# First attention of a fused model: value products in groups of four and five key tiles, tail keys padded to 128 rows, tail queries' maxima moved beside the tail keys' scores

## The reference

```python
# per batch of 8: N = 1056 tokens, nh = 8 heads, dh = 8
qkv = (x @ qkv_w + qkv_b).reshape(Bw, Nw, 3, nh, dh)
q, k, v = (qkv[:, :, 0], qkv[:, :, 1], qkv[:, :, 2])
attn = jnp.einsum('bnhd,bmhd->bhnm', q * scale, k)
bias = jnp.transpose(rpb_table[rel_idx], (2, 0, 1))
attn = jax.nn.softmax(attn + bias[None], axis=-1)
out = jnp.einsum('bhnm,bmhd->bnhd', attn, v).reshape(Bw, Nw, Cd)
```

## Time and profile before

| | us |
|---|---|
| median of 3 runs | 2691.78 |
| lowest, highest | 2688.55, 2697.84 |
| time of the profiled execution | 2689.29 |
| its span in the trace | 2687.5 |
| the attention stage in it | about 369 to 1223 |
| TensorE busy, of the span | 2455.1 (91%) |
| VectorE busy | 1911.8 (71%) |
| ScalarE busy | 1437.0 (53%) |

### The profile page before, as it was taken

One profiled execution on the slowest core, in us unless ns is written; L12 is line 12 of the kernel. 1 busy time (PEld: TensorE's weight loads), 2 busy tenths in 40 slices (PEclk: granted clock), 3 DMA queues, 4 the chain that ended last, 5 costly groups with the idle time before them and its releaser, 6 DMA issues. The chain is left out here.

```text
span 2687.5 us, 51435 instructions
## 1 busy us (share of the span) xinstructions
PE 2455.1 (91%) x18136; PEld 1069.5 (40%) x18136; DVE 1911.8 (71%) x4910; ACT 1437.0 (53%) x2468; POOL 394.1 (15%) x489
## 2 busy tenths in 40 slices
PE   8987689999999999997799997987799998799999
PEld 3336523333333333335333333666544444433333
DVE  4566688889888889873577776659677774366665
ACT  2117637777777777772344443427666765144333
POOL 2002100000000000005111112132101002311110
PEclk9997779999999999996899999666699999599999
DMA  2114511101010101306100000245612241600110
GB/s 92 24 32 155 194 30 27 37 26 37 25 37 25 37 25 37 61 9 130 28 21 22 22 22 22 65 106 159 226 45 84 64 98 43 138 16 17 32 25 12
DMA packets 233520, 155.14 MB, mean 58 GB/s; under 512 B 187617, under 2 KB 192546, under 8 KB 233042
## 3 DMA queue, kind: packets, MB, share of 16 engines
q1 hardware_dynamic: 220098, 123.57, 17.2%
q0 software_dynamic: 10368, 19.06, 2.5%
q10 hardware_dynamic: 2808, 9.22, 1.5%
HBM read 86.75 MB, written 65.09 MB: 57 GB/s over the span
## 5 line engine op out<-in xcount | busy, mean ns | idle before, releaser
L1666 DVE TENSOR_REDUCE att_mpart<-ps 128x1 f32<-128x512 f32 x1024 | 633.7, 683 | 55.7 <-PE ps L1486 50.6
L1624 ACT ACTIVATE att_p<-ps 128x704 f32<-128x704 f32 x768 | 546.5, 760 | 214.8 <-PE ps L1551 207.8
L1580 PE MATMUL ps<-att_p,att_v 128*9 128x352 f32 x3072 | 300.7, 462 | 0.1
L1486 PE MATMUL ps<-att_kT,att_qT 64*128 64x512 bf16 x1024 | 281.2, 386 | 20.9 <-DMA att_qz<-qt_d 8.4
L1551 PE MATMUL ps<-att_qT,att_kT 64*128 64x352 bf16 x1536 | 251.5, 317 | 7.3 <-ACT att_p L1624 6.9
L1280 DVE TENSOR_REDUCE cau_mpart<-ps 128x1 f32<-128x512 f32 (+5 forms) x384 | 193.1, 552 | 81.1 <-PE ps L1106 61.1
L2418 ACT ACTIVATE mo_act<-ps,mo_b 128x768 f32<-128x768 f32 x176 | 156.3, 901 | 132.0 <-PE ps L2300 127.4
L2571 DVE TENSOR_TENSOR mo_g<-mo_act,ps 128x768 f32<-128x768 f32 x176 | 167.4, 951 | 77.3 <-PE ps L2335 41.2
L1247 ACT ACTIVATE cau_p<-ps 128x704 f32<-128x704 f32 (+6 forms) x272 | 171.6, 660 | 82.3 <-PE ps L1165 49.7
L2970 ACT ACTIVATE mo_act<-ps 128x1024 f32<-128x1024 f32 (+1 forms) x108 | 102.9, 953 | 195.9 <-PE ps L2884 195.6
L1551 PEld LDWEIGHTS ps<-att_qT,att_kT 64*128 64x128 bf16 x1536 | 82.0, 93 | 272.9 <-issue 263.2
(11 more groups left out here) (419 smaller groups left out, 3928.9 us busy)
## 6 DMA issues: line engine op xcount, KB each, us to landing
qt_d<-pre_qT SPq DMA_DIRECT2D x8, 1056.0 KB, 4.3
kt_d<-pre_kT SPq DMA_DIRECT2D x8, 1056.0 KB, 7.3
att_kT<-kt_d SPq DMA_DIRECT2D x32, 264.0 KB, 2.8
att_qT<-qt_d SPq DMA_DIRECT2D x32, 264.0 KB, 3.0
cqt_d<-cpr_qT SPq DMA_DIRECT2D x8, 1056.0 KB
cau_qT<-cqt_d SPq DMA_DIRECT2D x16, 528.0 KB, 4.1
o_d<-att_o POOLq DMA_DIRECT2D x128, 37.1 KB, 2.7
cv_d<-cpr_v POOLq DMA_DIRECT2D x16, 288.0 KB, 6.0
```

Of the source, the lines that this page charges most:

```text
L1486: mm = pe.matmul(ps[:, bank, :], qT[half(s), u, j * P:(j + 1) * P], kT[half(s), u, c * BANK:(c + 1) * BANK], start=True, stop=not near)
L1580: mm = pe.matmul(ps[32 * cg:32 * cg + DV, 7, 0:TH], v[:, u, i, s, :], p[:, r, s, :], start=i < 2, stop=i == FULL - 1)
L1624: e = act.activation(p[:, n % PRING, :, :], ps[:, bank:bank + 2, 0:TH], ACT.Exp)
L1666: red = dve.tensor_reduce(mpart[:, j, s, c:c + 1], ps[:, bank, :], AX.X, ALU.max)
```

## The change

Groups of value products become (0,1,2,3) and (4,5,6,7,tail): 6 in a pair in place of 15. The buffer `p` gets nine slots in place of four. The tail keys' values are multiplied over all 128 rows: `vt` gets 128 partitions, and its lower half, and that of the one slot of `p` that the tail uses, are set to zero once by GpSimd (`blank`). The maxima of the tail queries move: the first one to the entry before the tail unit of the first third, the other two to the entries before the tail unit of the second; the tail keys' two go to the end of the list. The entries of a tail unit now run ahead of its scores, not behind. The numbers of entries behind each unit are written out (`sides`). The loops over batches become one loop over all 32 pairs, in which scores run ahead of values, and the copy of a third is left pending, across the ends of batches too. The copy of a third comes behind the first exponential of the fifth unit of the next third.

```diff
-    QT, MRING, PRING = 2, 3, 4
+    QT, MRING, PRING = 2, 3, 9
...
-    groups = [(t, [(t, i) for i in part]) for t in range(3) for part in ((0, 1), (2, 3), (4, 5), (6, 7), (None,))]
+    groups = [(t, [(t, i) for i in part]) for t in range(3) for part in ((0, 1, 2, 3), (4, 5, 6, 7, None))]
...
-    maxes += [("keys", s, 0, 0) for s in range(2)] + [("query", 0, 0, c) for c in range(3)]
+    maxes.insert(21, ("query", 0, 0, 0))
+    maxes += [("query", 0, 0, c) for c in range(1, 3)] + [("keys", s, 0, 0) for s in range(2)]
...
-    cut = [len(side) * c // NU for c in range(NU + 1)]
+    sides = (2, 1, 2, 1, 1, 2, 1, 1, 2) * 2 + (2, 1, 1, 3, 1, 1, 1, 1, 2)
+    cut = [sum(sides[:c]) for c in range(NU + 1)]
...
-        vt = nm.sb("vt", [64, U, 2, DV])
+        vt = nm.sb("vt", [P, U, 2, DV])
...
             pool.memset(mz[:, :, :, :], 0.0).then_inc(mz_set, 1)
+            pool.wait_ge(mz_set, 1)
+            pool.memset(vt[2 * TT:P, :, :, :], 0.0).then_inc(blank, 1)
+            pool.wait_ge(blank, 1)
+            pool.memset(p[2 * TT:P, PRING - 1, :, :], 0.0).then_inc(blank, 1)
+            pool.wait_ge(blank, 2)
...
-                    n = u * NU + first_unit[g] + c
-                    pe.wait_ge(p_made, it * U * NU + n - 1 if n >= 2 else it * U * NU)
+                    unit = first_unit[g] + c
+                    n = (it * U + u) * NU + unit
+                    if i is None:
+                        for pos in range(cut[unit], cut[unit + 1]):
+                            side_step(it, u, pos, last)
+                    at_least(pe, p_made, n - 1)
...
-                            mm = pe.matmul(ps[64 * s:64 * s + DV, 7, 0:TH], vt[:, u, s, :], p[0:2 * TT, r, 0, :], start=False,
+                            mm = pe.matmul(ps[64 * s:64 * s + DV, 7, 0:TH], vt[:, u, s, :], p[:, r, 0, :], start=False,
                                            stop=True)
...
+            start(0)
+            for k in range(pairs):
+                for g in range(NG):
+                    if g + 1 < NG:
+                        scores(k // U, k % U, g + 1, k >= pairs - U)
+                    elif k + 1 < pairs:
+                        start(k + 1)
+                    values(k // U, k % U, g)
...
-                            if n >= PRING:
-                                old = n - PRING
-                                act.wait_ge(pv_mm, it * U * NG + (old // NU) * NG + group_of[old % NU] + 1)
-                            else:
-                                act.wait_ge(pv_mm, it * U * NG)
+                            old = n - PRING
+                            if old >= 0:
+                                act.wait_ge(pv_mm, (old // NU) * NG + group_of[old % NU] + 1)
...
+                            if pending is not None and g % 2 == 1:
+                                out_third(*pending)
+                                pending = None
```

More of the change, by code:

```diff
@@ L1323, in attend_heads @@
     group_of = [n for n, (_, g) in enumerate(groups) for _ in g]
-    third_last = [5 * t + 4 for t in range(3)]
+    third_last = [2 * t + 1 for t in range(3)]
     maxes = [("full", s, j, c) for j in range(FULL) for c in range(2) for s in range(2)]
-    maxes += [("keys", s, 0, 0) for s in range(2)] + [("query", 0, 0, c) for c in range(3)]
+    maxes.insert(21, ("query", 0, 0, 0))
+    maxes += [("query", 0, 0, c) for c in range(1, 3)] + [("keys", s, 0, 0) for s in range(2)]
     NM = len(maxes)
@@ L1334, in attend_heads @@
     place = [(m - AHEAD if m >= AHEAD else side.index(("max", 2, m))) % MRING for m in range(NM)]
-    cut = [len(side) * c // NU for c in range(NU + 1)]
+    sides = (2, 1, 2, 1, 1, 2, 1, 1, 2) * 2 + (2, 1, 1, 3, 1, 1, 1, 1, 2)
+    cut = [sum(sides[:c]) for c in range(NU + 1)]
+    assert cut[NU] == len(side) and side[cut[9] - 1][2] == 21 and side[cut[18] - 1][2] == 34
     with ExitStack() as ctx:
@@ L1355, in attend_heads @@
         cdel = nm.sb("cdel", [P, 3, 160 * 8])
-        (set_up, mz_set, mrow_set, t_in, cor_rest, cor_hi, s_mm, p_made, pv_mm, o_cp, mx_mm, mx_red, m_row, m_hi, m_r1, m_mid,
+        (set_up, blank, mz_set, mrow_set, t_in, cor_rest, cor_hi, s_mm, p_made, pv_mm, o_cp, mx_mm, mx_red, m_row, m_hi, m_r1, m_mid,
          c_made, t_mm, t_cp) = nm.sems(
-            "set_up", "mz_set", "mrow_set", "t_in", "cor_rest", "cor_hi", "s_mm", "p_made", "pv_mm", "o_cp", "mx_mm", "mx_red", "m_row",
+            "set_up", "blank", "mz_set", "mrow_set", "t_in", "cor_rest", "cor_hi", "s_mm", "p_made", "pv_mm", "o_cp", "mx_mm", "mx_red", "m_row",
             "m_hi", "m_r1", "m_mid", "c_made", "t_mm", "t_cp")
@@ L1388, in load @@
                              (v[:, u, :, :, :], v_d[bi].rearrange("b p (u t s d) -> (b p) u t s d", u=U, t=NT, s=2)[:, u, :, :, :]),
[L1389 removed]
+                             (vt[0:2 * TT, u, :, :], vt_d[bi].rearrange("b p (h d) -> (b p) h d", d=DV)[:, 2 * u:2 * u + 2, :])):
                 sp.dma_start(dst, src).then_inc(loads[u], 16)
@@ L1559, in scores @@
                     mm.then_inc(s_mm, 1)
-                    for pos in range(cut[first_unit[g] + c], cut[first_unit[g] + c + 1]):
-                        side_step(it, u, pos, last)
+                    if i is not None:
+                        for pos in range(cut[unit], cut[unit + 1]):
+                            side_step(it, u, pos, last)
             def values(it, u, g):
                 t, parts = groups[g]
-                n0 = u * NU + first_unit[g]
-                if g % 5 == 0:
-                    pe.wait_ge(o_cp, (it * U + u) * 3 + t)
+                n0 = (it * U + u) * NU + first_unit[g]
+                if g % 2 == 0:
+                    at_least(pe, o_cp, (it * U + u) * 3 + t)
                 for c, (_, i) in enumerate(parts):
-                    pe.wait_ge(p_made, it * U * NU + n0 + c + 1)
+                    pe.wait_ge(p_made, n0 + c + 1)
                     r = (n0 + c) % PRING
                     if i is None:
-                        apart(pe, const)
+                        pe.wait_ge(blank, 2)
                     for s in range(2):
                         if i is None:
-                            mm = pe.matmul(ps[64 * s:64 * s + DV, 7, 0:TH], vt[:, u, s, :], p[0:2 * TT, r, 0, :], start=False,
+                            mm = pe.matmul(ps[64 * s:64 * s + DV, 7, 0:TH], vt[:, u, s, :], p[:, r, 0, :], start=False,
                                            stop=True)
@@ L1582, in values, with start @@
                 mm.then_inc(pv_mm, 1)
[L1584 to L1597, removed]
+            def start(k):
+                pe.wait_ge(t_cp, (k + 1) * QT)
+                scores(k // U, k % U, 0, k >= pairs - U)
+            start(0)
[6 more added lines that the diff above has]
+                    values(k // U, k % U, g)
         @block.scalar
@@ L1601, in _, with out_third, step @@
             enter(act, const, "act")
[L1602 to L1609, removed]
+            def out_third(it, u, t):
+                act.wait_ge(pv_mm, (it * U + u) * NG + third_last[t] + 1)
+                if t == 0:
+                    at_least(act, stored[u % 2], (it * (U // 2) + u // 2) * 64)
+                act.activation(o[:, u % 2, t * TH:(t + 1) * TH], ps[:, 7, 0:TH], ACT.Identity).then_inc(o_cp, 1)
+            def step(it, pending):
                 for u in range(U):
@@ L1612, in step @@
                         for c, (_, i) in enumerate(parts):
-                            n = u * NU + first_unit[g] + c
-                            act.wait_ge(s_mm, it * U * NU + n + 1)
-                            if n >= PRING:
-                                old = n - PRING
-                                act.wait_ge(pv_mm, it * U * NG + (old // NU) * NG + group_of[old % NU] + 1)
-                            else:
-                                act.wait_ge(pv_mm, it * U * NG)
+                            n = (it * U + u) * NU + first_unit[g] + c
+                            act.wait_ge(s_mm, n + 1)
+                            old = n - PRING
+                            if old >= 0:
+                                act.wait_ge(pv_mm, (old // NU) * NG + group_of[old % NU] + 1)
                             bank = 2 * (n % 2)
@@ L1625, in step @@
                             e.then_inc(p_made, 1)
-                        if pending is not None:
-                            out_third(*pending)
-                            pending = None
+                            if pending is not None and g % 2 == 1:
+                                out_third(*pending)
+                                pending = None
                         if g == third_last[t]:
-                            pending = (u, t)
-                out_third(*pending)
-            body(act, step)
+                            pending = (it, u, t)
+                return pending
+            pending = None
+            for it in range(IT):
+                pending = step(it, pending)
+            out_third(*pending)
         @block.vector
```

## The result

The changed kernel takes 2821.36 us (median of 4 runs, 2820.4 to 2825.22); the kernel before took 2690.62 in the same set of runs. The ratio is 1.0484, with a 95% interval of 1.0461 to 1.0506: 131 us slower. The profiled execution takes 2821.74 us, its span is 2819.9.

The account below looks back on a forecast made before the run. VectorE, starved of maxima behind long value groups, with TensorE waiting for banks, was taken as the bound: thirty beats from 26.72 to 31.0 us add 128, the last pair 5, so 133 and 2824 us; range 2715 to 2865.

Parts of the forecast that it names:

- The place that decides: Value group between products for the maxima: three banks just cover two tiles (gap 0.03 us); two more tiles add 0.60.
- The sizes of the pauses: VectorE idle behind each value group: 1.23 us for five, 0.90 for four; three of each make 6.4 us a pair.
- the round of the turns: Last third's round with tail keys' products, three maxima and two turns before the group of five: 6.4 us, not 4.8.
- The cover of 1.57 us: How long three full banks of maxima keep VectorE busy, from the start of the product that waited.
- The walk: TensorE's entries and groups followed through one third: 9.9 us, 29.8 for three, 31.4 a pair with corrections; 31.0 taken.
- Which ring: VectorE's three banks of maxima bound the pair; ScalarE, with 7.3 us a pair to lose, isn't the bound.
- Switches: Nine fewer value groups a pair, plus tail queries beside tail scores, save 2.5 us of TensorE's time; forecast to buy nothing.
- Only the groups of five starve: Rival: four-tile group with tail unit is covered; VectorE idles 3.7 us, pair 27.6 to 28, about 2729; chance 0.08.
- Switches decide: Rival, faster: TensorE's own time limits and VectorE stays fed; pair 26.6 to 24.1 us, total 2609; chance 0.10.
- Batch ends: The extra 0.79 us after every four pairs, seven times, goes: 5.5 us, included in the beat of 31.0.
- Last pair and start: Last pair, without maxima: ScalarE's two-bank cover gets short, 4 us, and the final group of five adds 1.2.
- The clock: Granted clock should stay 1.00; rival: it falls as TensorE pauses, up to 130 us on top, 2955; chance 0.04.

## Why the prediction was right

It said 2824 us, between 2715 and 2865, slower with a chance of 0.88; measured were 2821.

- *The place that decides.* A group of two tiles is just covered by three banks, a longer one isn't. Right: six pauses a pair, one for each group, and with the old lengths of groups the loss is gone.
- *The sizes of the pauses.* For groups of five I had 1.23, and more where the ring wasn't full; measured 1.11, 1.11, and 1.54 in the round of the turns. For groups of four I had 0.90 each; measured 0.64, 1.20 and 0.61. The cover of 1.57 us holds only where the last product waited for its bank and full reductions follow. In the first third the last product before the group of four went into a free bank (719.41), and VectorE's work lasts from there to 721.24: 1.83 us of cover, and a pause under my 0.90, so that 0.90 was no floor. In the second third the last two products are those of the tail queries, whose reductions are short (0.94 for both, 729.66 to 730.60), and the product behind the group is one for the tail keys, whose reduction starts 0.65 after it (731.15 to 731.80) in place of 0.43: hence 1.20. These errors cancel in part, and the whole idle time, 6.86, is near the 6.4.
- *The walk.* Round to the group of five: 4.83 for a measured 4.79. Round to the group of four: 5.1 for 4.90 in the second third, with two of the shorter products (731.15 less 726.25). The round with the turns: 6.4 for 6.31 (737.46 less 731.15). The sum was 31.4, I took 31.0, and it is 30.76; the first third's corner corrections were put too high: 5.1 + 0.5 for its round to the group of four, which takes 5.17 (30.72 less the other five rounds, of 4.79, 4.90, 6.31, 4.75 and 4.80).
- *Which ring.* Right that a reduction, not an exponential, ends a round: with the exponentials halved a pair is only 0.1 us shorter. What I left out is how near the second ring is; no number of the prediction hung on it, but the expectations for the halved reductions, for both halved, and for the first entries moved ahead on the changed kernel failed by it.
- *Switches.* The 2.5 us of TensorE's time that I gave them buy nothing while TensorE waits for banks. Its busy time by marks fell by only 0.3 a pair, and the two rivals "Only the groups of five starve" and "Switches decide" both lost. (The latter is what the prediction means where it writes "the second rival's"; it is the first of its list.) The Trainium skill, "TensorEngine Tiling (Array Packing)", has both sides: its Key Properties say that a change of tiling mode drains the engine, its PSUM Bottleneck that the emptying of PSUM may become the limit. Here the second decided, by the 6.86 us of VectorE's idle time beside 4.69 of TensorE's.
- *Batch ends.* 5.5 us predicted; the one loop alone brings 4.9 (0.3 to 7).
- *Last pair and start.* I had 5.2 for the last pair and the end, and it is 1.9. I had nothing for the start, where 5.7 us more go, and I counted thirty beats where the first pair grows too, by 4. So the 133 of the sum (128 + 5) met the 132.4 of the span (121 + 4 + 5.7 + 1.9) by errors that cancel. That the beat is right to 0.3 us is the mechanism; that the time is right to 3 us is in part luck.
- *The clock.* Stayed at 1.00 in the pair's window, as predicted, but not throughout: in the beat to pair 30, which takes 31.51 us, it is 0.89.

What stays open: why five groups a third with the new placing (2698) lose 10 us to the old placing; only the placing as a whole was tried.

## What to carry to other kernels

When one in-order engine feeds two others through rings of banks, measure the time from the last item before a long block to the first behind it, and compare it with what the full ring covers; blocks longer than that make the feeder wait before them and the fed engine behind them. Fewer, longer blocks are worth having only up to that length: here three banks and steps of 0.60 us carried groups of two tiles, and of two tiles and the tail. And a second ring can stand so close behind the one that limits that halving the work behind either alone shows little of its size (0.1 and 1.9 us a pair here, 4.0 together): halve both.

## What the runs showed of the hardware that was not expected

In the run with three groups a third the granted clock fell in some pairs of the stage, although TensorE is marked busy for 26.1 of the 27.6 us of an ordinary one. The pair whose window shows 0.94 took 28.78 us in place of 27.55:

```profile
541.43:570.21 28.78, 27.36 (x248) 9.43 (x251) 23.78 (x48) 19.30 (x31) 1.99 (x4) 0.94 0.11 29
570.21:597.76 27.55, 26.13 (x248) 9.33 (x251) 23.77 (x48) 19.29 (x31) 2.00 (x4) 1.00 0.11 31
```

In it the clock is at the lower of its two levels, 0.50, in the windows from 555 to 558 us; in the three us before that TensorE is marked busy for 2.34. Such pairs add about 8 us to this run. The changed kernel, in which TensorE is marked idle three times as long, shows 1.00 in an ordinary pair, but in the beat to the store of pair 30 the clock falls there too, to 0.50 from 1324 to 1330 us:

```profile
1301.68:1333.19 31.51, 24.56 (x219) 8.69 (x218) 13.57 (x31) 18.96 (x31) 1.99 (x5) 0.89 0.03 6
```

Single pairs at 0.94 or 0.95, 1.3 to 1.6 us longer than the others, stand also in the three runs with halved work. What makes the difference between such a pair and its neighbours was not tried.
